# Self attention's key product by seven products of 2x2 blocks, and the order of the work around it

## What is computed

```python
q = tgt @ in_proj_w[:D].T + in_proj_b[:D]
k = tgt @ in_proj_w[D:2 * D].T + in_proj_b[D:2 * D]
v = tgt @ in_proj_w[2 * D:].T + in_proj_b[2 * D:]
scores = jnp.einsum('btd,bsd->bts', q, k) / jnp.sqrt(jnp.float32(D))
attn = jax.nn.softmax(scores, axis=-1)
sa = jnp.einsum('bts,bsd->btd', attn, v) @ out_proj_w.T + out_proj_b
x = _ln(tgt + sa, g1, be1)
```

## Time and profile before

| | us |
|---|---|
| three runs | 511.86, 511.75, 511.29; median 511.75 |
| the profiled execution | 512.02, its span 510.1 |
| TensorE busy | 503.7 of 510.1 |
| VectorE, ScalarE, GpSimd busy | 374.3, 242.7, 137.5 |

### The profile page before, as it was taken

How to read it: one execution, slowest core, us unless ns; L and a number is a source line. 1 busy time by engine, 2 the same in 40 slices (tenths; PEclk the granted TensorE clock), 3 DMA queues, 4 the chain that set the end, 5 groups by cost and what they waited for, 6 DMA issues and landing times.

```text
span 510.1 us, 7640 instructions
## 1 busy us (share of the span) xinstructions
PE 503.7 (99%) x2958; PEld 485.2 (95%) x2958; DVE 374.3 (73%) x644; ACT 242.7 (48%) x429; POOL 137.5 (27%) x104
## 2 busy tenths in 40 slices
PE   8999999999999999999999999999999999999997
PEld 6899999899988888999999999999999899999996
DVE  4853769786799896787699777368586878796645
ACT  3853652465598876164644334206536632442210
POOL 2430541014023134154504000444438313030000
PEclk9999999999999999999999999999999999999999
DMA  8951122031689961213521242002202022202004
GB/s 222 349 206 59 60 84 82 1 116 59 225 287 325 318 219 49 82 25 123 125 82 66 89 159 84 1 1 75 91 2 82 2 84 82 84 0 84 2 0 130
DMA packets 18508, 53.76 MB, mean 105 GB/s; under 512 B 1704, under 2 KB 2504, under 8 KB 15912
## 3 DMA queue, kind: packets, MB, share of 16 engines
q1 hardware_dynamic: 18412, 53.21, 31.5%
q10 hardware_dynamic: 60, 0.07, 0.1%
HBM read 51.63 MB, written 1.64 MB: 104 GB/s over the span
## 4 chain that ended last, share of the span: by engine, by line
PE 97%; DMA 1%; SPq 1%; DVE 0%; issue 0%; ACT 0%; DVEq 0%
PE ps L808 18%; PE ps L810 18%; PE ps L809 18%; PE ps L872 5%; PE ps L871 5%; PE ps L870 5%; PE ps L926 3%; PE ps L900 2%; PE ps L1067 2%; PE ps L1068 2%; PE ps L1069 2%; PE ps L1041 2%; PE ps L1043 2%; PE ps L1042 2%; DMA OR<-wvo_in 1%; PE ps L1013 1%
## 5 line engine op out<-in xcount | busy, mean ns | idle before, releaser
L808 PE MATMUL ps<-AH,WH 128*128 128x400 f32 x284 | 98.5, 347 | 0.0
L810 PE MATMUL ps<-AH,WL 128*128 128x400 f32 x284 | 98.0, 345 | 0.0
L809 PE MATMUL ps<-AL,WH 128*128 128x400 f32 x284 | 97.9, 345 | 0.0
L808 PE MATMUL ps<-XH,WH 128*128 128x400 f32 x192 | 66.7, 347 | 0.0
L810 PE MATMUL ps<-XH,WL 128*128 128x400 f32 x192 | 66.3, 345 | 0.0
L809 PE MATMUL ps<-XL,WH 128*128 128x400 f32 x192 | 66.2, 345 | 0.0
L651 POOL TENSOR_TENSOR WL<-WR,WH 128x512 fp32r<-128x512 f32 x29 | 41.4, 1457 | 69.8 <-ACT WH L1233 69.8
L808 PEld LDWEIGHTS ps<-AH,WH 128*128 128x128 f32 x284 | 53.4, 188 | 0.2
L809 PEld LDWEIGHTS ps<-AL,WH 128*128 128x128 f32 x284 | 53.4, 188 | 0.0
L810 PEld LDWEIGHTS ps<-AH,WL 128*128 128x128 f32 x284 | 53.4, 188 | 0.0
L1233 ACT ACTIVATE WH<-WR 128x512 fp32r<-128x512 f32 x60 | 34.1, 624 | 25.5 <-DMA WR<-wts_in 25.5
(11 more groups left out here) (245 smaller groups left out, 1195.6 us busy)
## 6 DMA issues: line engine op xcount, KB each, us to landing
WR<-wts_in SPq DMA_DIRECT2D x19, 1024.0 KB, 4.8
ctR<-ctxt_in SPq DMA_DIRECT2D x16, 722.0 KB, 6.7
cnR<-ctxn_in SPq DMA_DIRECT2D x16, 512.0 KB, 4.9
cnR<-ctxn_in SPq DMA_DIRECT2D x8, 256.0 KB
tok<-x_in SPq DMA_DIRECT2D x8, 192.0 KB, 8.6
tok<-x_in SPq DMA_DIRECT2D x1, 1536.0 KB
cnR<-ctxn_in SPq DMA_DIRECT2D x8, 160.0 KB
VR<-wvo_in SPq DMA_DIRECT2D x4, 256.0 KB, 6.4
```

The source lines that it names most:

```text
L808: pe.matmul(dst, wh, half(mh, h, k), start=(k == 0), stop=False)
L809: pe.matmul(dst, wh, half(ml, h, k), start=False, stop=False)
L810: mm = pe.matmul(dst, wl, half(mh, h, k), start=False, stop=(k == KC - 1))
```

## The change

The key product is made by seven products of 2x2 blocks. The weight `WRK` is seen as four blocks of 256 x 256 (a11 to a22), the features as b11, b21 (half 0) and b12, b22 (half 1). GpSimd makes s1 = a21 + a22, s2 = s1 - a11, s4 = a12 - s2, s3 = a11 - a21 right behind the load, with `inverse_deviation(1, 1)` between the second and the third; then the sums `X0` = XH + XL of half 0, and later t3 and t4. VectorE makes t1 and t2 from the transposes in PSUM. All seven blocks and four feature sums are split into high and low. A product is two groups of six matmuls. Products 0 and 1 take the place of U_K half 0, products 2 to 5 stand behind U_Q half 1, product 6 behind `self_scores(0)`. VectorE puts the products together into `kT` (`key_add`), where ScalarE evacuated `kT` before.

Moved with it: `self_prob_transpose(0)` stands right ahead of `self_attend(0)`; ScalarE splits S_CQ in one stretch behind `self_normalise(0)`, and `ct(0, 1)` behind `self_normalise(1)`; VectorE's `split_ct(0, 0)` and `split_ct(0, 1)` and the second half of `bias_product(u_q)` stand behind `self_normalise(1)`; GpSimd splits S_CQ only after the first scores; `load_cn(0)` waits for the last addition into `kT`. The diff, cut to its core:

```diff
@@ sync
             def load_cn(b, pieces=range(3)):
                 if b == 0:
-                    wait_w_low(sp, U_K, KC // 2 - 1)
-                    wait_w_low(sp, U_K, KC - 1)
+                    sp.wait_ge(k_out, 8)
@@ gpsimd
-            for k in range(KC // 2, KC):
-                pool.wait_ge(w_high, KC * WHOLE.index(U_K) + k + 1)
-                pool.tensor_tensor(WL[SLOT[U_K]][:, k, :], WRK[:, k, :], raw(WH[SLOT[U_K]][:, k, :]),
-                                   ALU.subtract).then_inc(wk_low_pool, 1)
+            a11, a12, a21, a22 = [raw_key_block(*at) for at in ((0, 0), (1, 0), (0, 1), (1, 1))]
+            s2, s3, s1, s4 = [key_block(i)[2] for i in range(3, 7)]
+            pool.wait_ge(wk_loaded, 16)
+            pool.tensor_tensor(s1, a21, a22, ALU.add).then_inc(k_sum, 1)
+            pool.wait_ge(k_sum, 1)
+            pool.tensor_tensor(s2, s1, a11, ALU.subtract).then_inc(k_sum, 1)
             inverse_deviation(1, 1)
-            pool.wait_ge(vo_made, KC)
+            pool.wait_ge(k_sum, 2)
+            pool.tensor_tensor(s4, a12, s2, ALU.subtract).then_inc(k_sum, 1)
+            pool.tensor_tensor(s3, a11, a21, ALU.subtract).then_inc(k_sum, 1)
+            pool.wait_ge(x_ready, KC)
+            for i in range(2):
+                ks = slice(2 * i, 2 * i + 2)
+                pool.tensor_tensor(X0[:, ks, :], raw(XH[0][:, ks, :]), raw(XL[0][:, ks, :]), ALU.add).then_inc(k_x0, 1)
+            pool.wait_ge(k_tsum, 2)
+            pool.wait_ge(k_x0, 2)
+            t2, t3, t4, t1 = [key_sums(t)[2] for t in range(4)]
+            pool.tensor_tensor(t3, t2, X0[:, 0:2, :], ALU.subtract).then_inc(k_tsum_pool, 1)
+            pool.tensor_tensor(t4, t2, X0[:, 2:4, :], ALU.subtract).then_inc(k_tsum_pool, 1)
+            pool.wait_ge(s_scores, 1)
             for t in (ctH[0], ctL[0]):
                 pool.memset(t[:, :, M:724].bitcast(F32), 0.0).then_inc(pads_set, 1)
             split_weights(S_CQ)
@@ tensor: key_products
+                        for k in range(2):
+                            pe.matmul(dst, ah[:, k, cols], bh[:, k, :], start=(k == 0), stop=False)
+                            pe.matmul(dst, ah[:, k, cols], bl[:, k, :], start=False, stop=False)
+                            mm = pe.matmul(dst, al[:, k, cols], bh[:, k, :], start=False, stop=(k == 1))
+                        mm.then_inc(gemm_done, 1)
@@ tensor: order
             unit(U_Q, 0)
-            unit(U_K, 0, [0])
+            key_products([0])
             to_features(0, 1, tiles[1])
-            unit(U_K, 0, [1, 2, 3])
+            key_products([1])
             unit(U_Q, 1)
+            key_products([2, 3, 4, 5])
             self_scores(0)
-            unit(U_K, 1)
-            self_prob_transpose(0)
+            key_products([6])
             combine_bias()
             self_scores(1)
+            self_prob_transpose(0)
             self_attend(0)
             unit(U_VO, 0, [0, 1, 2])
             self_prob_transpose(1)
@@ scalar: order
-            for k in range(KC):
-                split_weights(U_K, k)
+            split_key(0)
+            split_key(1)
+            split_key(2)
             unit(U_Q, 0, [0, 1, 2])
             normalise(0, 1, tiles[1])
             unit(U_Q, 0, [3])
-            unit(U_K, 0, [0])
+            split_key(3)
+            act.wait_ge(k_sum, 4)
+            act.wait_ge(k_low, 3)
+            for e in range(2):
+                act.wait_ge(gemm_done, key_done(0, e))
+                act.activation(kmid[:, e, :], ps[:, KEY_BANKS[0] + e, 0:HALF], ACT.Copy).then_inc(k_first, 1)
             norm_features(0, 1)
-            unit(U_K, 0, [1, 2, 3])
+            for i in (4, 5, 6):
+                split_key(i)
+            split_key_sum(0)
+            unit(U_Q, 1, [0])
+            split_key_sum(3)
+            unit(U_Q, 1, [1])
+            split_key_sum(1)
+            split_key_sum(2)
+            unit(U_Q, 1, [2, 3])
+            self_exp(0)
             split_ct(0, 0)
-            unit(U_Q, 1)
-            self_exp(0)
-            split_ct(0, 1)
-            unit(U_K, 1, [0])
             self_normalise(0)
-            unit(U_K, 1, [1, 2, 3])
+            for k in range(KC):
+                split_weights(S_CQ, k)
             self_probT(0)
             self_exp(1)
             self_attended(0)
             self_normalise(1)
+            split_ct(0, 1)
             unit(U_VO, 0, [0, 1, 2])
             self_probT(1)
@@ vector: order
-            split_weights(U_K, 0)
-            split_weights(U_K, 1)
+            split_key(0)
+            split_key(1)
+            split_key(2)
             normalise(0, 1, tiles[1])
+            split_key(3)
             norm_features(0, 1)
+            dve.tensor_tensor(t1, ps[:, 4:6, 0:HALF], X0[:, 0:2, :], ALU.subtract).then_inc(k_tsum, 1)
+            dve.wait_ge(k_tsum, 1)
+            dve.tensor_tensor(t2, ps[:, 6:8, 0:HALF], t1, ALU.subtract).then_inc(k_tsum, 1)
+            for e in range(2):
+                dve.wait_ge(k_first, e + 1)
+                key_add(1, e, half(kT, 0, e), kmid[:, e, :], k_out, col=e)
+            for i in (4, 5, 6):
+                split_key(i)
+            split_key_sum(0, 1)
+            split_key_sum(3, 2)
+            split_key_sum(1, 3)
+            split_key_sum(2, 4)
...
-            unit(U_K, 0)
-            split_ct(0, 0)
-            unit(U_Q, 1)
-            bias_product(u_o, OR, C_BV, None, u_o_ready)
...
+            self_max(0)
+            for e in range(2):
+                dve.wait_ge(k_four, e + 1)
+                key_add(6, e, half(kT, 1, e), kmid[:, e, :], k_out, col=e)
+            self_normalise(0)
...
-            self_max(0)
-            self_normalise(0)
-            split_ct(0, 1)
-            bias_product(u_q, WR, C_CBK, S_CQ, u_q_ready)
...
             self_max(1)
+            bias_product(u_q, WR, C_CBK, S_CQ, u_q_ready, [0, 1])
             self_attended(0)
             self_normalise(1)
+            bias_product(u_q, WR, C_CBK, S_CQ, u_q_ready, [2, 3])
+            split_ct(0, 0)
+            split_ct(0, 1)
             dve.wait_ge(vob_ready, 1)
             unit(U_VO, 0, [0, 1])
             bias_product(u_k, WR, C_CBQ, S_CK, u_k_ready, [0])
```

More of the change, by code:

```diff
@@ L41 @@
 LOADED = [n for n in range(NU) if n not in (U_VO, U_A)]
-KINDS = (["fp32", "fp32", "residual", None, None, "split", "residual"]
+KINDS = (["fp32", "key", "residual", None, None, "split", "residual"]
          + ["relu_bias", "down_residual"] + ["relu_bias", "down_add"] * (NF - 1)
@@ L98 @@
 HANDED = [(0, 0), (0, 1), (0, 2), (0, 3), (1, 2), (1, 3), (1, 0), (1, 1)]
-WHOLE = [n for n in LOADED if n not in STRASSEN]
+WHOLE = [n for n in LOADED if n not in STRASSEN and n != U_K]
 assert all(POS[n, 0] > at for at, n in SPLIT_AT.items() if n in LAST)
@@ L117, in dve_writes @@
 def dve_writes(n):
-    return KINDS[n] not in ("fp32", "down_first")
+    return KINDS[n] not in ("fp32", "key", "down_first")
 def groups(n, h):
-    if n not in STRASSEN:
+    if n not in STRASSEN and n != U_K:
         return KC
-    first = 2 if n == PARTED else 5
+    first = 2 if n in (PARTED, U_K) else 5
     return 2 * first if h == 0 else PRODUCTS - 2 * first
@@ L419, in wait_w_low @@
                 before -= 1
-            if n == U_K and k >= KC // 2:
-                eng.wait_ge(wk_low_pool, k - KC // 2 + 1)
-                return
-            if n not in (U_Q, U_K):
+            if here and n != U_Q:
                 before -= KC // 2
@@ L456, in sums, with key_block, raw_key_block, key_sums @@
             return TH[:, 2 * t:2 * t + 2, :], lo, whole
+        def key_block(i):
+            if i >= 4:
+                return [w[:, i - 4, :, :] for w in (KXH, KXL, KXS)]
+            ks, es = [(0, 0), (2, 0), (2, D // 2), (0, D // 2)][i]
+            return [w[SLOT[U_K]][:, ks:ks + 2, es:es + D // 2] for w in (WH, WL, WS)]
+        def raw_key_block(ks, es):
+            return WRK[:, 2 * ks:2 * ks + 2, es * D // 2:(es + 1) * D // 2]
+        def key_sums(t):
+            lo, whole = [w[0][:, 2 * t:2 * t + 2, :] if t < 3 else w[1][:, :, :]
+                         for w in ((TL[0], KTL), (TS[0], KTS))]
+            if t == 0:
+                whole = KT2[:, :, :]
+            return TH[:, 2 * t:2 * t + 2, :], lo, whole
+        def key_done(i, e):
+            return gemm_count(U_K, 0, 2 * i + e) if i < 2 else gemm_count(U_K, 1, 2 * (i - 2) + e)
+        KEY_BANKS = [0, 2, 4, 6, 0, 2, 6]
         def product(n, i, e):
@@ L873, in strassen, with key_products, b @@
                         mm.then_inc(gemm_done, 1)
+            def key_products(products):
+                def b(h, k):
+                    return XH[h][:, k:k + 2, :], XL[h][:, k:k + 2, :]
+                moving = [b(0, 0), b(0, 2)] + [key_sums(t) for t in range(4)] + [b(1, 2)]
+                for i in products:
+                    block_of = [0, 1, 3, 4, 2, 5, 6][i]
+                    ah, al = key_block(block_of)[:2]
+                    bh, bl = moving[i][:2]
```

(47 more changed lines are left out.)

79 lines of the change are left out of this document (62 added, 17 removed).

## The result

| | before | after |
|---|---|---|
| median of 5 runs, us | 511.86 (511.29 to 512.26) | 531.59 (530.84 to 532.60) |
| ratio | | 1.0387, 95% interval 1.0375 to 1.0399 |
| span of the profiled execution | 510.1 | 529.5 |

The account below looks back on a forecast made before the run. It took TensorE's matmul count times spacing as the bound (busy 503.7 of 510.1 us). Terms -2.2 + 0.8 + 1.2 + 6.9 + 3.0 = +9.7 us gave 521.5 us on the median, range 516.0 to 526.0.

Parts of the forecast that it names:

- second wait: At `self_attend(0)`: TensorE waits for ScalarE's copy of the transposed probabilities to `sprobT`; +1.2 us (0.75 to 1.4).
- third wait: At `self_attend(1)`: S_CK's late load holds ScalarE's splits and the `sprobT` copy; +6.9 us (4.2 to 8.5).
- Rival 1: At `self_attend(1)`: the load of S_CK is hidden and the change pays, 511.5 or 510.3 us; chance 0.08.
- first wait: At the second half's normalisation: `nmr` and `tok` meet GpSimd's sums, delaying the transposes; +0.8 us, up to +3.0.
- Rival 3: At the second half's normalisation: GpSimd's sums win every turn against `tok`, +2.2 on top, 523.7 us; chance 0.20.
- The tail: Behind the S_CK stall: VectorE's lateness, 1.2 us, and TensorE's lower clock, 1.8; together +3.0 us (0.5 to 5).
- The saving: In the key product: twelve fewer matmuls at 0.184 us each, all on TensorE's path; -2.2 us.

Follow-up runs that it names:

- a2: The changed kernel with GpSimd waiting for its own previous sum ahead of each of the four sums; 526.51 us in a single run.
- c1: The changed kernel with unused matmuls filling TensorE's two long gaps (31 ahead of the second half's transposes, 41 ahead of `self_attend(1)`); 529.40 us, ratio 1.0331.
- b1: The changed kernel with SyncE issuing the load of S_CK ahead of the two loads of ct(1); 523.95 us, ratio 1.0227.
- k0: The kernel before with only twelve matmuls of the key product left out, at less precise keys; 510.59 us, ratio 0.9986.
- g4: g1 with the softmax stage and VectorE's order re-laid, GpSimd's last two block sums behind `tok`, first feature sum split earlier; 512.12 us, ratio 1.0006.
- g1: b1 with all four block sums ahead of the power, feature sums behind `tok`, and `tok` ahead of two key splits on VectorE; 516.90 us, ratio 1.0087.
- a1: The changed kernel with GpSimd's s4, s3 and the two X0 sums starting only when the second half's `tok` is normalised; 526.88 us, ratio 1.0277.
- a3: The changed kernel with GpSimd's power widened from 100 to 128 partitions and the sums left back to back; 528.96 us in a single run.

## Why the prediction was wrong

**Right.** The twelve matmuls, the three waits and whom they name, and the chain to the third. With S, the moment at which `self_scores(0)` was issued, at 63.14, the steps stand so:

| | predicted | in the trace of after |
|---|---|---|
| `self_attend(0)` | S+7.5 | S+7.8 (70.89) |
| last `QL` done | S+12.3 | S+12.7 |
| second context split done | S+17.1 | S+17.4 (80.51) |
| S_CK issued | S+17.5 | S+17.9 (81.03) |
| landed | S+24.4 | S+25.6 (88.78) |
| `self_attend(1)` | S+27.1 | S+28.3 (91.41) |
| second wait, third wait | 1.2, 6.9 | 1.1, 7.6 |

Of the steps between, only the landing is off by more than 0.4: 7.7 us in place of 6.9. The wait of 7.6 is inside its bound (8.5). Rival 1 was rightly given little.

**The step that failed** is the first wait's: "`nmr` then meets s4 [...] So `nmr` comes at 30.6", priced at 0.8 us with a worst case of 3.0. It was 5.8, and 2.4 of halved clock came behind it, 8.2 in all: 7.4 of the 10.1 us by which the forecast missed. Up to 29.1 the step was right (the power's end was predicted for 29.3). It went by one row, in which a small operation lost to one GpSimd sum and got in behind it, and took that for the rule at each turn. a2 shows that this rule holds when the sums have gaps, at 32.31 for the predicted 32.4. In after the sums were all free to run, and behind a power on 100 partitions the small operation got no turn. Rival 3 (a chance of 0.20) had the right kind of failure and a price of 2.2, since it too let `nmr` in behind s4. The trace of before couldn't give this price: its VectorE operations that meet GpSimd operations back to back (the `u_q` steps above) get in at the first boundary, and none of them stands behind a power on 100 partitions. But the upper bound could have been the end of all the sums that were ready, 35.2, in place of two of them.

**The tail** was mis-sized: 3.0 for VectorE's lateness and the clock, 4.2 measured behind the third wait, at a clock of 0.50. The term was put at 1.8 for the clock and 1.2 for VectorE, added up. The 1.8 were worked out from the kernel's first matmuls as a stretch at the lower clock; the profile has a granted clock of 1.00 there (1.7 to 6.2 us), so that row doesn't show what the clock costs, and that the size came near is luck. c1 and b1 show that they don't add: VectorE's 1.6 us at the `XS` bank come out when the clock is up, and lie under the slow matmuls when it is down. What was left out is that the first wait has a clock term too; at the predicted 0.8 us it had none, and behind a2's 1.2 us of idle time there was none either. The Trainium skill, "TensorE: Matmul & The Clock Gate", section "HAM oscillation — how this bites in real kernels", cited in the prediction, says that a long idle gap between bursts puts the engine back to 1.2 GHz; after agrees, with 0.50 behind 5.8 and behind 7.6 us.

**The saving**, -2.2, was right on TensorE and would have been too much as a gain: k0 keeps 1.1 of it, because ScalarE's cover at `kT` was short by 0.9, and g4 none, because VectorE got more work where it was nearly full. "What another engine does costs nothing as long as it is early enough" was right as a sentence; I didn't read off how early each one was.

**Open**: 1.0 us of the 19.4 isn't given to a cause (0.4 between the waits, 0.6 behind 100.8), and why the run of sums let VectorE in nowhere in after is only argued.

## What to carry to other kernels

Where a small VectorE operation on the path is released by GpSimd, look at what GpSimd has queued behind the releaser and free to run: bound the wait by the end of the whole run, and put the run behind the small operation's consumer, or a wait between its parts. A load whose buffer comes free late belongs at the head of its queue, since a place behind another transfer costs twice, at the issue and at the landing (4.0 and 3.0 us here). And before counting matmuls saved, read how much slack the engines around them have: here ScalarE was 0.9 us short at one copy, and work moved to VectorE ate the rest of the gain.

## What the runs showed of the hardware

- A VectorE operation on four columns stood for 6.13 us against four GpSimd sums back to back. The same operation took 1.25 us when the sums had gaps, and also 1.25 us with no gaps when the GpSimd operation ahead of them was 128 partitions wide and not 100.
- The granted clock fell without a long stall too. Behind the 1.6 us wait for `XS` it was 0.50 from 84 to 86 us in g1, from 95 to 98 in c1 and from 89 to 95 in b1. In g4, with no wait over 0.5 us in that stretch, it stayed at 1.00.
- In a1 and a2 it was 0.50 from 106 to 108 us as well, some 20 us behind the last stall and with no idle time in TensorE's rows of the 10 us before. No run shows what brings this fall about.
- Behind the transposes' 1.2 us of idle time in a2 it stayed at 1.00 (32 to 43 us), and behind their 2.9 us in a3 it was 0.83 over the next 10 us, with 0.50 from 36 to 38.
- VectorE's steps of 128x512 with two inputs in SBUF took 1.65 us in turns with GpSimd's back-to-back splits in the kernel before, and 0.75 without them.
